# The first batch of an attention and mixture-of-experts layer: keys read in halves, maxima's rows sent ahead of the next stack reads on two queues and transposed a round later, fourth buffers cleared by GpSimd

## What is computed

```python
qkv = x @ W_qkv.T + b_qkv                      # x: (32, 256, 128), 16 heads of 8
att = jnp.einsum('bthd,bshd->bhts', q, k) / math.sqrt(hs)
att_prob = jax.nn.softmax(att, axis=-1)
att_v = jnp.einsum('bhts,bshd->bthd', att_prob, v)
x = _layernorm(x + att_v @ W_out.T + b_out)
scores = sigmoid(x @ gate_w.T)                 # the two highest of 8, with expert_bias
out = shared(x) + sum over the two experts e of score * (silu(r @ w1[e].T) * (r @ w3[e].T)) @ w2[e].T
x = _layernorm(x + out)
```

## Time and profile before

| | us |
|---|---|
| median of 3 runs | 765.87 |
| lowest, highest | 764.38, 766.14 |
| profiled execution | 764.94 |
| its span, first to last instruction | 763.1 |
| TensorE busy | 740.5 (97%) |
| VectorE busy | 630.9 (83%) |
| ScalarE busy | 521.4 (68%) |
| GpSimd busy | 500.8 (66%) |
| mean granted TensorE clock | 0.98 |

### The profile page before, as it was taken

The page is one execution under the profiler, slowest core; times in us unless marked ns, Lnnn a source line. Parts: engine busy times, 40 slices in busy tenths (PEclk is TensorE's granted clock), DMA queues, the critical chain, the costliest instruction groups (busy, mean ns, idle before and its releaser), DMA issues.

```text
span 763.1 us, 20494 instructions
## 1 busy us (share of the span) xinstructions
PE 740.5 (97%) x7004; PEld 531.6 (70%) x7004; DVE 630.9 (83%) x1353; ACT 521.4 (68%) x1069; POOL 500.8 (66%) x714
## 2 busy tenths in 40 slices
PE   4899999999999999999999999999999999999996
PEld 2456665665666566566554788888888888888886
DVE  6889999999999999999997657988666766666676
ACT  3289899998988889898888646454454544455442
POOL 7356888878777787877624755566565655655564
PEclk8599999999999999999999999999999999999999
DMA  6667666675665556656611745454554544455440
GB/s 171 179 160 190 182 174 185 169 191 162 168 172 156 172 148 169 171 160 174 154 32 43 203 116 115 118 130 117 152 128 128 126 127 129 129 125 124 125 106 29
DMA packets 202369, 108.93 MB, mean 143 GB/s; under 512 B 10537, under 2 KB 202281, under 8 KB 202281
## 3 DMA queue, kind: packets, MB, share of 16 engines
q1 hardware_dynamic: 198560, 105.22, 52.9%
q10 hardware_dynamic: 3720, 2.57, 1.4%
HBM read 73.41 MB, written 33.82 MB: 141 GB/s over the span
## 4 chain that ended last, share of the span: by engine, by line
PE 93%; DVE 2%; DMA 1%; issue 1%; ACT 1%; POOL 1%; ACTq 0%; POOLq 0%; SPq 0%; DVEq 0%
PE bank L1037 17%; PE bank L841 16%; PE bank L810 11%; PE bank L848 9%; PE bank L849 9%; PE bank L850 9%; PE bank L826 8%; PE bank L934 3%; PE bank L904 3%; PE bank L958 2%; PE bank L965 1%; PE bank L990 1%; DVE negmax L1188 1%; PE bank L869 1%; PE bank L974 1%
## 5 line engine op out<-in xcount | busy, mean ns | idle before, releaser
L1188 DVE TENSOR_REDUCE negmax<-bank 128x2 f32<-128x512 f32 x512 | 322.9, 679 | 16.1 <-PE bank L826 13.7
L666 ACT ACTIVATE probs<-bank 128x512 f32<-128x512 f32 x512 | 294.2, 613 | 47.7 <-PE bank L810 43.8
L784 ACT ACTIVATE q_stack<-k_stack 128x512 f32<-128x512 f32 x128 | 80.8, 631 | 152.3 <-DVE k_stack L1247 152.1
L826 PE MATMUL bank<-k_stack,q_stack 48*128 48x256 bf16 x1024 | 163.5, 281 | 8.8 <-DMA q_stack<-q_parts_dram 6.1
L810 PE MATMUL bank<-q_stack,k_stack 50*128 50x256 bf16 x1024 | 157.7, 274 | 0.7 <-ACT probs L666 0.4
L1247 DVE TENSOR_TENSOR k_stack<-bank,probs 128x512 f32<-128x512 f32 x128 | 88.3, 689 | 71.0 <-PE bank L850 69.5
L841 PE MATMUL bank<-probs,v_aug 128*32 128x256 f32 x2048 | 137.6, 386 | 0.2 <-ACT attT L677 0.2
L848 PE MATMUL bank<-x_hi,hi_w 128*128 128x512 f32 x288 | 126.5, 439 | 1.3 <-DVE res L1200 0.5
L810 PEld LDWEIGHTS bank<-q_stack,k_stack 50*128 50x128 bf16 x1024 | 75.9, 95 | 72.2 <-issue 35.3
L849 PE MATMUL bank<-x_hi,lo_w 128*128 128x512 f32 x288 | 114.2, 396 | 0.0
L850 PE MATMUL bank<-x_lo,hi_w 128*128 128x512 f32 x288 | 113.7, 395 | 0.0
(11 more groups left out here) (132 smaller groups left out, 1198.2 us busy)
## 6 DMA issues: line engine op xcount, KB each, us to landing
probs<-route_dram SPq DMA_DIRECT2D x128, 256.0 KB, 5.0
k_stack<-k_parts_dram SPq DMA_DIRECT2D x64, 192.0 KB, 4.1
q_stack<-q_parts_dram SPq DMA_DIRECT2D x62, 192.0 KB, 3.4
q_parts_dram<-q_parts SPq DMA_DIRECT2D x32, 192.0 KB, 2.1
k_parts_dram<-k_parts SPq DMA_DIRECT2D x32, 192.0 KB, 2.2
k_parts_dram<-k_parts SPq DMA_DIRECT2D x32, 128.0 KB, 2.0
q_parts_dram<-q_parts SPq DMA_DIRECT2D x32, 128.0 KB, 2.1
x_sb<-x SPq DMA_DIRECT2D x32, 128.0 KB, 2.2
```

Of the source, the lines that this page charges most:

```text
L666: nc.scalar.activation(probs[h][:], score_ps[bank(b, h)][:].rearrange("p (j t) -> p j t", j=NT), ACT.Exp).then_inc(exp_done, 1)
L784: nc.scalar.activation(act[n % DEPTH], gated[n % DEPTH] if n else up1_ps[0][:], ACT.Silu).then_inc(act_set, 1)
L826: mm = pe.matmul(max_ps[bank(b, h)][:, i * T:(i + 1) * T], q_stack[b.ring][first:last, h // 2, i * P:(i + 1) * P], k_stack[b.ring][first:l ...
L1188: nc.vector.tensor_reduce(negmax[b.ring % 2][:, :, column], max_ps[bank(b, head)][:].rearrange("p (i s) -> p i s", i=NT), AX_X, ALU.max, n ...
```

## The change

1. **Keys in halves.** `first_stack` reads batch 0's keys with four DMAs in place of two, first both of heads 0 to 7, then both of heads 8 to 15, on semaphores `first_k_in[0]` and `[1]`. TensorE waits for the first before head 0 and for the second before head 8.
2. **The rows of batch 0 ahead.** In slot -1, SyncE waits for `max_rows` and sends the rows at the head of the slot, ahead of batch 4's load and batch 2's stack reads (`row_maxima_in`). It sends only the first half; the second is issued by ScalarE, at the end of its slot -1. All later batches keep the old place and both DMAs on SyncE.
3. **A round later.** For batch 0, TensorE's transposes move from round 4 to round 5, and VectorE's copy from step 9 to step 11.
4. **The fourth buffers.** GpSimd clears `k_stack[3]` and `v_aug[3]` behind its constants, VectorE only the first three. SyncE and ScalarE wait for `fourth_set` for the fourth.

```diff
--- before.py
+++ after.py
@@ -138,13 +138,15 @@
         c_in, bv_out, expert_in = sem("c_in"), sem("bv_out"), [[sem(f"expert_in{m}_{n}") for n in range(0, NE, 3)] for m in range(3)]
         q_split_set = sem("q_split_set")
         wqk_hi_set, wqk_lo_set, xT_hi_set, xT_lo_set = (sem(n) for n in ("wqk_hi_set", "wqk_lo_set", "xT_hi_set", "xT_lo_set"))
+        fourth_set = sem("fourth_set")
         k_ones, v_clear, consts_set = sem("k_ones"), sem("v_clear"), sem("consts_set")
         bqs_set = sem("bqs_set")
         q_mm, k_mm, v_mm = sem("q_mm"), sem("k_mm"), sem("v_mm")
         qk_f = sem("qk_f")
         split_step, parts_out = sem("split_step"), sem("parts_out")
         stack_in = [sem(f"stack_in{r}") for r in range(RING)]
-        first_k_out, first_q_out, first_k_in = sem("first_k_out"), sem("first_q_out"), sem("first_k_in")
+        first_k_out, first_q_out = sem("first_k_out"), sem("first_q_out")
+        first_k_in = [sem(f"first_k_in{n}") for n in range(2)]
         first_q_in = [sem(f"first_q_in{n}") for n in range(2)]
         max_in = [sem(f"max_in{r}") for r in range(RING)]
         v_set = sem("v_set")
@@ -340,9 +342,12 @@
             def first_stack(b):
 
                 sp.wait_ge(first_k_out, 16 * PARTS)
-                for u in range(2):
-                    sp.dma_start(k_stack[b.ring][HALF * u:HALF * u + ROWS, :, :],
-                                 k_parts_dram[b.ring].rearrange("(g u) d c t -> u (d c) g t", u=2)[u]).then_inc(first_k_in, 16)
+                for n in range(2):
+                    pairs = slice(n * PAIRS // 2, (n + 1) * PAIRS // 2)
+                    for u in range(2):
+                        sp.dma_start(k_stack[b.ring][HALF * u:HALF * u + ROWS, pairs, :],
+                                     k_parts_dram[b.ring].rearrange("(g u) d c t -> u (d c) g t", u=2)[u][:, pairs, :]).then_inc(first_k_in[n], 16)
+
             def k_part_out(b, part, signal):
 
                 first, count = QPART.index(part), QPART.count(part)
@@ -370,13 +375,24 @@
                 sp.wait_ge(q_split_set, 3)
                 q_part_out(b, 2, first_q_out)
 
+            def row_maxima_in(b):
+                sp.wait_ge(max_rows_set, b.count(1, 1))
+                for u in range(2 if b.c else 1):
+                    sp.dma_start(q_stack[b.ring][HALF * u + ROWS:HALF * u + ROWS + 2, :, :],
+                                 max_rows[H * u:H * u + H, :]).then_inc(max_in[b.ring], 16)
+
             def slot(t):
+                if t.neg.c == 0:
+                    row_maxima_in(t.neg)
                 b = t.stack
                 if b.live and b.later(RING):
 
                     sp.wait_ge(score_mm, b.count(H, H * (1 - RING)))
                 elif b.live:
-                    sp.wait_ge(k_ones, b.c + 1)
+                    if b.c < RING - 1:
+                        sp.wait_ge(k_ones, b.c + 1)
+                    else:
+                        sp.wait_ge(fourth_set, 1)
                 b = t.load
                 if b.live and b.later(3):
                     if b.later(RING) and not t.stack.later(RING):
@@ -391,12 +407,8 @@
                         for u in range(2):
                             sp.dma_start(stack[b.ring][HALF * u:HALF * u + ROWS, :, :],
                                          dram[b.ring].rearrange("(g u) d c t -> u (d c) g t", u=2)[u]).then_inc(stack_in[b.ring], 16)
-                b = t.neg
-                if b.live:
-                    sp.wait_ge(max_rows_set, b.count(1, 1))
-                    for u in range(2):
-                        sp.dma_start(q_stack[b.ring][HALF * u + ROWS:HALF * u + ROWS + 2, :, :],
-                                     max_rows[H * u:H * u + H, :]).then_inc(max_in[b.ring], 16)
+                if t.neg.live and t.neg.c:
+                    row_maxima_in(t.neg)
                 b = t.soft
                 if b.live:
                     if b.later(2):
@@ -472,6 +484,14 @@
             columns = ident[:].rearrange("p (g w) -> p g w", w=32)
             pool.tensor_copy(used_first[:, 0:4 * W].rearrange("p (g w) -> p g w", w=W), columns[:, :, 0:W]).then_inc(consts_set, 1)
             pool.tensor_copy(used_first[:, 4 * W:P].rearrange("p (g w) -> p g w", g=4), columns[:, :, W:32]).then_inc(consts_set, 1)
+
+            r = RING - 1
+            pool.memset(k_stack[r][:].rearrange("p h t -> p (h t)").bitcast(F32), TWO_ONES).then_inc(fourth_set, 1)
+            pool.memset(v_aug[r][:], 0.0).then_inc(fourth_set, 1)
+            pool.wait_ge(fourth_set, 2)
+            for u in range(2):
+                ins = pool.memset(v_aug[r][:, :, u, :, 2 * D + u:2 * D + u + 1], 1.0)
+            ins.then_inc(fourth_set, 1)
 
             def split_x(g, r):
                 pool.wait_ge(x_hi_set, g + 1)
@@ -700,8 +720,10 @@
                             act_e.wait_ge(v_mm, b.count(1, 1))
                         if b.later(RING):
                             act_e.wait_ge(av_mm, b.count(4, 4 * (1 - RING)))
+                        elif b.c < RING - 1:
+                            act_e.wait_ge(v_clear, 2 * (b.c + 1))
                         else:
-                            act_e.wait_ge(v_clear, 2 * (b.c + 1))
+                            act_e.wait_ge(fourth_set, 3)
                         for u in range(2):
                             nc.scalar.activation(
                                 v_aug[b.ring][:, :, u, :, D * u:D * u + D],
@@ -755,6 +777,9 @@
                             for n in range(0, NE, 3):
                                 if t.soft.c == expert_slot(m, n):
                                     load_expert(m, n)
+                if t.neg.c == 0:
+                    act_e.wait_ge(max_rows_set, 1)
+                    act_e.dma_start(q_stack[0][HALF + ROWS:HALF + ROWS + 2, :, :], max_rows[H:2 * H, :]).then_inc(max_in[0], 16)
                 if t.proj.c == 2:
                     load_constants()
                 if t.proj.c == 3:
@@ -815,7 +840,7 @@
             def row_maxima_scores(b, h, i):
 
                 if i == 0 and b.c == 0 and h in (0, H // 2):
-                    pe.wait_ge(first_k_in, 32)
+                    pe.wait_ge(first_k_in[h // (H // 2)], 32)
                     pe.wait_ge(first_q_in[h // (H // 2)], 32)
                 elif i == 0 and h == 0:
                     pe.wait_ge(stack_in[b.ring], b.lap(64, 64 if b.ring else 0))
@@ -965,7 +990,7 @@
                             mm = pe.matmul(gate_ps[:, i, :], x1T_new[:, i * P:(i + 1) * P], gate_sb[:], start=True, stop=True)
                         mm.then_inc(gate_mm, 1)
                     b = t.neg
-                    if b.live and p == PE_TOK:
+                    if b.live and p == (PE_TOK if b.c else PE_TOK + 1):
 
                         pe.wait_ge(max_lo_set, b.count(1, 1))
                         if b.c == 0 and not b.looped:
@@ -1090,10 +1115,9 @@
             dve.wait_ge(q_split_set, 2)
             nc.vector.tensor_tensor(q_split[:, 2, :], rq[:], q_split[:, 1, :], ALU.subtract).then_inc(q_split_set, 1)
             clear_values(1)
-            for r in (2, 3):
-                clear_keys(r)
-                clear_values(r)
-            dve.wait_ge(v_clear, 2 * RING)
+            clear_keys(2)
+            clear_values(2)
+            dve.wait_ge(v_clear, 2 * (RING - 1))
 
             step = [0]
 
@@ -1210,15 +1234,17 @@
                             dve.wait_ge(tok_T, t.tail.count(1, 1))
                         if t.gated.live:
                             dve.wait_ge(gate_mm, t.gated.count(1, 1))
-                        if t.neg.live:
+                        if t.neg.live and t.neg.c:
                             dve.wait_ge(max_T, t.neg.count(1, 1))
                     b = t.tail
                     if b.live and h == DVE_TOK:
                         v = tok_ps.rearrange("p (a w) -> p a w", w=W)
                         nc.vector.reciprocal(recip_sum[:], v[:, :, 2 * D:W]).then_inc(recip_set, 1)
                     b = t.neg
-                    if b.live and h == DVE_TOK:
-
+                    if b.live and h == (DVE_TOK if b.c else DVE_TOK + 2):
+
+                        if b.c == 0:
+                            dve.wait_ge(max_T, 1)
                         if b.later(1):
                             prev = Batch(b.i, b.c - 1, B)
                             dve.wait_ge(max_in[prev.ring], prev.lap(32, 32))
```

## The result

| | before | after |
|---|---|---|
| median of 6 runs, us | 765.87 | 769.12 |
| lowest, highest | 764.38, 766.14 | 768.20, 769.59 |
| profiled execution, us | 764.94 | 768.51 |
| its span, us | 763.1 | 766.7 |

The ratio is 1.0047, with a 95% interval of 1.0036 to 1.0057. The change costs 3.3 us by the medians and 3.6 us by the two profiled executions. One execution of one kernel further down (both DMAs on SyncE) took 1393.24 us, for a reason that no run here shows; it is not in that kernel's ratio.

What follows compares the result with a forecast made beforehand. TensorE, 93% of the chain, was taken as the bound, so delay before L810 moves the end: rows 30.36, load landed 33.65, ScalarE's DMA landed 37.1, hence +4.8 us; 769.7 or, from the median, 770.7, middle 770.2 us, range 767.3 to 773.3.

Steps and rivals of the forecast that it cites:

- L810 as the yardstick: First score matmul of batch 0, at 32.27 us before; what moves it was said to move the end.
- Halves: Start of the maxima: four smaller key reads win 0.2 us, bounds -1.7 to +0.3, the query read being last.
- The later round: Slot before batch 0's scores: two more reductions precede the copy, so the rows are ready 1.1 us later.
- From rows to load: SyncE, slot -1: from the rows being ready at 30.36 to issuing batch 4's load at 31.15, 0.7 us for the row DMA.
- The load's landing: Batch 4's xT load, issued by SyncE behind the rows: 2.5 us to land, at 33.65, releasing xT_hi.
- ScalarE's DMA: Row DMA of the second half, issued at 33.7 behind xT_hi: 3.4 us to land, at 37.1.
- GpSimd's clears: GpSimd before L484: clears of 1024 elements take about 0.9 us each, hidden, so they cost 0.
- Which hides it: SyncE's queue: batch 1's parts leave some 0.9 us later, hidden by its wait for batch 1's query parts.
- B: Rival: ScalarE's row DMA goes out with SyncE's, scores -0.8 to +1.2 us, 765.1 in the middle; chance 0.09.
- C: Rival: maxima starting before 13.0 us keep the clock at 2.4 GHz, net -3.1 us, 761.8 us; chance 0.03.
- Rival D: GpSimd's clears run at the two-input pace, 2.2 us more, 771.9 us; chance 0.05.
- E: Rival: the clock rises 3 us later after L810, costing 1.5 us, 771.2 us; chance 0.08.

Runs made afterwards that it cites:

- both DMAs on SyncE: The changed kernel with both row DMAs of batch 0 sent from SyncE and none from ScalarE; median 765.91 us, ratio to before 1.0010.
- held parts: The kernel before, with SyncE waiting until batch 0's keys have landed before it writes batch 1's parts; 766.02 us, a single execution.
- round only: The kernel before with only batch 0's transposes moved to round 5 and the copy to step 11; median 765.90 us, ratio 1.0012.
- load first: The changed kernel with batch 4's load put back ahead of SyncE's wait for the rows; median 764.52 us, ratio to before 0.9995.
- VectorE clears: The changed kernel with batch 4's load ahead of the rows' wait, transposes in round 4, and fourth buffers cleared by VectorE; 764.18 us, ratio 0.9988.
- late half: The changed kernel with batch 4's load ahead of the rows' wait, transposes in round 4, keys' second half behind batch 1's key parts; 763.81 us, 0.9983.
- ScalarE's DMA first: The changed kernel with ScalarE's row DMA moved ahead of xT_hi in its program; median 765.54 us, ratio to before 1.0005.
- halves and GpSimd only: The kernel before with only the keys in halves and GpSimd's clearing of the fourth buffers; median 765.23 us, ratio 1.0007.
- order only: The kernel before with only the rows' place changed: SyncE sends the first half ahead, ScalarE the second; median 770.01 us, ratio 1.0054.

## Why the prediction was right, point by point

**The direction, the mechanism and the place** were right: the row DMA behind `xT_hi` behind the load behind the rows. The sum gave +4.8 us, 770.2 us; measured were +3.6 us in the profile and 769.12 us, inside the range. L810 as the yardstick held here: it moved by 3.63 us and the profiled execution by 3.57.

**The sizes**, term by term. *Halves*: taken 0.2 us won, measured 1.24, the one large miss. The step that failed was the assumption that the engines share themselves between the two queues as before; the kernel with held parts and the halves show that keys already issued hold the queries. The bound of 1.7 held; the +0.3 on the other side had no row behind it, and no kernel showed such a cost. The prediction named a first maxima matmul before 14 as a sign of being wrong. It came at 14.02, and in four later kernels with the same halves at 13.82 to 13.98, so passing that mark was luck. *The later round*: forecast 1.1 us, measured 1.0 in the change and alone. *From rows to load*: 0.8 forecast, 0.96 measured. *The load's landing*: 2.5 taken, 2.07 measured, a little below the lowest row. *ScalarE's DMA*: 3.4 taken, 3.66 to the matmul. The misses come to -1.2 us: -1.5 from the halves and the load, +0.3 from the rest.

**GpSimd's clears** were right, 0 us. The row that was missing before is there now, 0.95 us each against my 0.9 from the slope of small ones:

```profile
2.25 0.95 POOL L489 MEMSET k_stack<- 128x1024 f32 x1
...
3.13 0.95 POOL L490 MEMSET v_aug<- 128x1024 f32 x1
...
5.89 0.67 POOL L504 TENSOR_TENSOR k_parts<-kf,k_parts 128x256 bf16<-128x256 f32 x1 [1.58 <-ACT kf L745]
```

L504 starts 0.14 us later than L484 did, but behind `kf`, with 1.58 us of idle time before it, so the clears didn't delay it. Rival D fell. Here the Trainium skill's GPSIMD Engine Reference, section 4.1 "Engine selection", agrees in its first half, one-input work at roughly line rate: GpSimd's 0.95 us (0.88 from start to start) stand beside VectorE's 0.91 us for the same clear.

**SyncE's later work, costed at nothing.** "Which hides it" was wrong as a statement on the halves: batch 1's parts went out later, and with these two parts alone SyncE's stack reads of batch 2 slipped by 1.5 us against the kernel before (0.7 against "round only"), and the rows behind them came late, which took back what the halves had won. In the changed kernel it costs nothing, since the rows no longer stand behind those reads, so the sum didn't suffer. It also shows what sending the rows ahead is good for.

**The rivals.** B fell: the order bites, as three kernels show that take it away. C did not come up, since the maxima began at 14.0 and the granted clock had fallen at 13.2. What it rests on is doubtful besides: in load first, VectorE clears and late half TensorE began the maxima at 13.88, 13.82 and 14.15 with the granted clock at 1.00, ran three heads, waited for VectorE, and the clock fell all the same, at 15.0, 14.8 and 15.3. The time of the fall lies between 12.1 and 15.3 us in the twelve profiled executions, so 13.0 was the number of one. E fell, too. The granted clock rises at 43.9 us in the changed kernel (0.54 in the row from 43.0 on), 8.0 us after the first score matmul, and that distance was 8.0 us before as well:

```profile
43.00:44.00 1.00, 1.00 (x16) 0.34 (x8) 0.52 (x1) 0.64 (x2) 0.32 (x2) 0.54 0.01 3
```

**The second queue** is worth little, as the Trainium skill's DMA: Bandwidth & Descriptors says under "Issuing engines are not separate DMA queues": both on SyncE, the scores come 0.35 us later behind the maxima than with ScalarE's DMA first (17.97 against 17.62, one profiled execution each).

## What to carry to other kernels

Before a DMA is moved to another engine's queue, read that engine's program upwards from the new place: it leaves only when every wait above it has been met (here at 32.24 us, with the rows ready at 29.18), and one of those may hang on the very queue that was to be relieved. When a wait is moved ahead of other issues on a queue, each of these inherits it, so ask of each who waits for it; the load of a later batch looked idle and held ScalarE. And a read started earlier is worth its time only if the queue that carries the next link is not later by it.

## What was not expected of the hardware

- A DMA of 8 KB took 1.9 us to land with no reads near it (round only), 2.4 beside the first of the stack reads (load first), 3.0 and 3.1 right behind them (parts held, halves and GpSimd only), 3.6 and 4.7 us in their midst (the change, order only). Its size says little; what was issued just before it, also on the other queue, goes with most of the spread, but not with the 1.1 us between the last two.
- The clock can rise 3 us apart behind nearly the same work. In eleven of the twelve profiled executions the granted clock rises 7.1 to 8.7 us after the first score matmul, in "ScalarE's DMA first" 11.7 us after it. That kernel and "both on SyncE" do the same work in slot 0, with waits that differ by half a microsecond, the latter's first key product being 0.2 us earlier (34.22 against 34.41), and the granted clock rises at 43.4 in the one and at 40.4 us in the other:

```profile
43.00:44.00 1.00, 1.00 (x14) 0.51 (x17) 1.00 (x4) 0.92 (x3) 1.00 (x2) 0.79 1.20 203
```

```profile
40.00:41.00 1.00, 1.00 (x16) 0.36 (x12) 0.85 (x2) 0.97 (x3) 0.07 (x1) 0.80 0.06 20
```

Three microseconds more at 1.2 GHz are about 1.5 us of the end, by estimate. The first kernel's profiled execution took 766.62 us, 1.1 above its median, which would fit a difference between two executions of one kernel; that is not shown, each kernel having one profile, and no run here shows what decides it.
